# A four-layer kernel: maxima spread by load, first keys moved by other queues, five products a quarter slot later

## What is computed

```python
x = x + cross_attention(layernorm(x), ctx, tau, delta)   # 16 heads of 16, ctx has 1601 rows
x = x + top1_of_8_experts(layernorm(x))                   # router, all 8 experts, the best one kept
x = x + window_attention(ctx, layernorm(x))               # scores in a window, context, tanh(cat @ W_c.T)
x = x + slots(layernorm(x))                               # gelu, top 8 of 64 slots, slots updated once

# cross attention:
scores = einsum('blhe,bshe->bhls', qh, kh) * tau + delta
a = softmax(scores / sqrt(16)); out = einsum('bhls,bshd->blhd', a, vh) @ Wo.T + bo
```

## Time and profile before

| | us |
|---|---|
| three runs | 1069.53, 1071.1, 1069.47 |
| median | 1069.53 |
| the profiled execution | 1072.81 |
| its span, first to last instruction | 1070.8 |
| TensorE busy in it | 980.2 (92%) |
| VectorE busy | 742.4 (69%) |
| ScalarE busy | 572.9 (54%) |
| GpSimd busy | 64.5 (6%) |

### The profile page before, as it was taken

How to read it: one execution, slowest core, us unless ns; L and a number is a source line. 1 busy time by engine, 2 the same in 40 slices (tenths; PEclk the granted TensorE clock), 3 DMA queues, 4 the chain that set the end, 5 groups by cost and what they waited for, 6 DMA issues and landing times.

```text
span 1070.8 us, 13621 instructions
## 1 busy us (share of the span) xinstructions
PE 980.2 (92%) x4794; PEld 389.6 (36%) x4794; DVE 742.4 (69%) x1704; ACT 572.9 (54%) x1063; POOL 64.5 (6%) x91
## 2 busy tenths in 40 slices
PE   7699999999899999889899989889899989889886
PEld 3353322233333334323333334323333334234643
DVE  5589888887777777767677687777677774126633
ACT  3366666666455456656455456656455466740330
POOL 3351000000000000000000000000000000100000
PEclk9899999999999999989899999999899899899899
DMA  7946500001000000001000000001000000040032
GB/s 190 190 88 112 123 1 16 16 2 35 1 16 1 15 1 11 6 1 55 1 16 1 16 1 13 4 1 55 1 16 1 1 1 21 21 127 1 1 98 79
DMA packets 34411, 36.19 MB, mean 34 GB/s; under 512 B 6766, under 2 KB 31387, under 8 KB 34083
## 3 DMA queue, kind: packets, MB, share of 16 engines
q1 hardware_dynamic: 33102, 34.43, 13.1%
q10 hardware_dynamic: 1162, 0.64, 0.4%
q0 software_dynamic: 80, 0.26, 0.1%
HBM read 21.55 MB, written 7.35 MB: 27 GB/s over the span
## 4 chain that ended last, share of the span: by engine, by line
issue 48%; PE 31%; DVE 8%; DMA 4%; SPq 3%; ACT 2%; POOL 2%; DVEq 1%; POOLq 0%; ACTq 0%
PE ps_o L1168 8%; PE ps_m L1084 8%; PE ps_e L1370 5%; DVE mx L1671 4%; DMA xres<-in_x 1%; PE ps_e L1041 1%; PE ps_m L1370 1%; SPq L558 1%; DMA q_stack<-probs 1%; PE ps_m L1188 1%; DMA d_parts<-delta_parts 1%; PE ps_m L1318 1%; POOL rstd L701 1%; POOL xres L753 1%; ACT probs L867 1%
## 5 line engine op out<-in xcount | busy, mean ns | idle before, releaser
L1671 DVE TENSOR_REDUCE mx<-ps_m 128x1 f32<-128x401 f32 x1024 | 536.1, 568 | 186.0 <-PE ps_m L1084 177.4
L867 ACT ACTIVATE probs<-ps_e 128x512 f32<-128x512 f32 (+1 forms) x763 | 438.3, 598 | 325.1 <-PE ps_e L1370 323.2
L1084 PE MATMUL ps_m<-k_stack,q_stack 99*128 99x401 bf16 x1024 | 318.6, 343 | 36.5 <-DVE mx L1671 27.0
L1370 PE MATMUL ps_e<-q_stack,k_stack 101*128 101x512 bf16 (+1 forms) x763 | 298.6, 393 | 11.2 <-ACT probs L867 9.4
L1168 PE MATMUL ps_o<-probs,v_heads 128*32 128x512 f32 (+1 forms) x1664 | 232.2, 632 | 0.0
L1370 PEld LDWEIGHTS ps_e<-q_stack,k_stack 101*128 101x128 bf16 (+1 forms) x763 | 75.5, 100 | 264.6 <-ACT probs L867 172.4
L1084 PEld LDWEIGHTS ps_m<-k_stack,q_stack 99*128 99x128 bf16 x1024 | 101.6, 99 | 183.0 <-DVE mx L1671 123.5
L1272 PE MATMUL ps_m<-expert_w,xnT 128*128 128x512 f32 x192 | 98.4, 593 | 0.7 <-DVE xb L1809 0.7
L1168 PEld LDWEIGHTS ps_o<-probs,v_heads 128*32 128x32 f32 (+1 forms) x1664 | 33.4, 109 | 62.7 <-issue 49.8
L867 ACT ACTIVATE probs<-ps_m 128x512 f32<-128x512 f32 (+1 forms) x69 | 41.5, 601 | 15.6 <-PE ps_m L1370 15.6
L1809 DVE SCALAR_TENSOR_TENSOR xb<-ps_m,hot,xb 128x256 f32<-128x256 f32 x84 | 40.6, 483 | 7.8
(11 more groups left out here) (333 smaller groups left out, 730.7 us busy)
## 6 DMA issues: line engine op xcount, KB each, us to landing
q_stack<-q_parts SPq DMA_DIRECT2D x78, 64.0 KB, 2.6
expert_w<-in_expert_wT SPq DMA_DIRECT2D x2, 1024.0 KB, 12.9
xres<-in_x SPq DMA_DIRECT2D x4, 512.0 KB, 3.8
x<-xres SPq DMA_DIRECT2D x4, 512.0 KB, 3.0
probs<-x SPq DMA_DIRECT2D x1, 2048.0 KB, 8.7
...
```

Of the source, the lines that this page charges most:

```text
L867: act.activation(probs[0:n, k % 2, h, :], score_bank(c, k, h)[0:n, :], ACT.Exp).then_inc(s["exp_done"], 1)
L1084: pe.matmul(ring_bank((n1, u))[:, 0:SPLIT], qst[0:MAX_ROW, g, h, P * t:P * t + P], kst[0:MAX_ROW, HG * g + h, QUARTER_START[q]:QUARTER_STA ...
L1370: pe.matmul(score_bank(c, k, h)[0:n, :], kst[0:ROWS, HG * g + h, P * st:P * st + n], qst[0:ROWS, g, h, :], start=True, stop=True).then_inc ...
L1671: dve.tensor_reduce(mx[:, q, col:col + 1], ring_bank((n1, u))[:, 0:SPLIT], AX.X, ALU.max)\
```

## The change

It has three parts.

1. **Maxima by load.** `units_of` gets the chunk. Chunk 0 keeps the even spread; chunks 1 to 3 take the table `BY_LOAD`, 2 to 7 units a slot, still 256 in all, and `BY_QUARTER` splits them over the quarters. `max_end`, `units_at` and `M_AT` follow. In chunks 1 to 3 the groups' turned maxima come in quarters 45, 89, 145 and 193 (before: 45, 97, 149 and 201).
2. **Five products later.** The lags of `y0`, `router`, `score0`, `z0` and `h` go from 3 to 4, and all that follows a job moves with it: `e0` from quarter 38 to 40, `t2a` from 117 to 119, `aTa` from 137 to 140, `t3a` from 170 to 174, `logits` from 181 to 186, `alphaT` from 199 to 204.
3. **The first keys' moves.** SyncE loses the ones, the delta's store and the delta's load; ScalarE issues the store behind step `D`; GpSimd issues the ones of the queries, the delta's load, and two of the six row moves of the first and the second key piece; ScalarE keeps none of these two. The ones of the maximum rows go on GpSimd inside the loop, behind step `L` 2. The masks go from the end of `START` to unit 8 of the loop.

```diff
-GATHER_SP = ((0, 4, 2, 1, 5, 3), (0, 4, 2, 1), (0, 4, 2))
-GATHER_ACT = ((), (5, 3), (1, 5, 3))
+GATHER_SP = ((0, 4, 2, 1), (0, 4, 2, 1), (0, 4, 2))
+GATHER_POOL = ((5, 3), (5, 3))
+GATHER_ACT = (1, 5, 3)
...
-         ("K", 3, 0), ("V", 0), ("V", 1), ("G", 2)]
-START += [("V", i) for i in range(2, V_EARLY)] + [("L", 1), ("U",)]
-BESIDE = []
+         ("K", 3, 0), ("V", 0), ("V", 1), ("G",)]
+START += [("V", i) for i in range(2, V_EARLY)] + [("L", 1)]
+BESIDE = [(8, ("U",))]
...
+BY_LOAD = [4, 5, 3, 5, 7, 2, 2, 7, 7, 2, 7, 4, 7,
+           7, 5, 4, 6, 6, 6, 6, 6, 6, 6, 6, 4, 6,
...
+BY_QUARTER = {2: (1, 0, 1, 0), 3: (1, 0, 1, 1), 4: (1, 1, 1, 1), 5: (1, 2, 1, 1), 6: (1, 2, 1, 2), 7: (2, 2, 1, 2)}
...
-JOBS = [("ota", None, 10, 3), ("otb", "ota", 2, 3), ("y0", "otb", 3, 3), ("y1", "y0", 2, 3), ("t1a", "y1", 11, 3),
-        ("t1b", "t1a", 2, 3), ("router", "t1b", 3, 2), ("e0", "router", 5, 6)]
+JOBS = [("ota", None, 10, 3), ("otb", "ota", 2, 3), ("y0", "otb", 4, 3), ("y1", "y0", 2, 3), ("t1a", "y1", 11, 3),
+        ("t1b", "t1a", 2, 3), ("router", "t1b", 4, 2), ("e0", "router", 5, 6)]
...
-            sp.wait_ge(s["delta_parts"], 1)
-            sp.dma_start(d_parts.rearrange("a (p s) -> p a s", s=P), delta3[:]).then_inc(s["delta_stored"], 16)
-            sp.wait_ge(s["delta_stored"], 16)
...
+            pool.wait_ge(s["delta_stored"], 16)
+            pool.dma_start(kst[DELTA_ROW:DELTA_ROW + 3, 0:3 * HG, :], d_parts[:, 0:S].unsqueeze(1).broadcast_to((3, 3 * HG, S)))\
+                .then_inc(s["ld_delta_k"], 16)
+            for i, rows in enumerate(GATHER_POOL):
+                first_col, end_col, last_block = KEY_PIECES[i]
+                pool.wait_ge(s["blk_parts"], BLOCK[last_block] + 1)
+                for j, row in enumerate(rows):
+                    move_k(pool, 0, (row,), k_soft[len(rows) * i + j], first_col, end_col)
```

More of the change, by code:

```diff
@@ L182, in ring_numbers @@
             k, h = divmod(q, HG)
-            order += [(NG * c + j, u) for j, u in units_at(k, h) if wanted(NG * c + j)]
-            if q in M_AT and wanted(NG * c + 1 + M_AT.index(q)):
-                order.append(("m", NG * c + 1 + M_AT.index(q)))
+            order += [(NG * c + j, u) for j, u in units_at(c, k, h) if wanted(NG * c + j)]
+            if q in M_AT[c] and wanted(NG * c + 1 + M_AT[c].index(q)):
+                order.append(("m", NG * c + 1 + M_AT[c].index(q)))
             if q in O_AT and (c or q > O_AT[0]):
@@ L401, in build @@
         k_half = [sem(f"k_half{i}") for i in range(2)]
+        k_soft = [sem(f"k_soft{i}") for i in range(4)]
         q_loaded = [sem(f"q_loaded{g}") for g in range(NG)]
@@ L528, in block_cols, with wait_first_keys @@
             return k_cols[BLOCKS[b][1]][1] if BLOCKS[b][0] == "K" else CT
+        def wait_first_keys(eng, half):
+            if half == 0:
+                eng.wait_ge(k_half[0], 16 * sum(len(rows) for rows in GATHER_SP[:2]))
+                for moved in k_soft:
+                    eng.wait_ge(moved, 16)
+            else:
+                eng.wait_ge(k_half[1], 16 * K_PARTS)
         def k_loads(g):
@@ L628, in _ @@
                 sp.wait_ge(q_stored[m], 16 * NC)
-            for i, half in enumerate(k_half):
-                sp.wait_ge(half, 16 * K_PARTS * HALF_OF_PIECE.count(i))
+            for i in range(2):
+                wait_first_keys(sp, i)
             sp.wait_ge(k_loaded[1], 16 * K_PARTS)
@@ L1894, in chunk @@
                     for h in range(HG):
-                        for j, u in units_at(k, h):
+                        for j, u in units_at(c, k, h):
                             if wanted(NG * c + j):
```

62 lines of the change are left out of this document (33 added, 29 removed), and 2 rows, old and new, of the table BY_LOAD.

## The result

| | before | after |
|---|---|---|
| median of 20 runs, us | 1070.22 | 1064.60 |
| ratio of the runs, 95% interval | 1 | 0.9933 [0.9913, 0.9953] |
| the profiled execution, us | 1072.81 | 1067.79 |
| before chunk 0, us | 89.6 | 94.3 |
| chunks 0, 1, 2, 3, us | 160.2, 237.8, 238.0, 224.8 | 161.0, 231.9, 231.9, 225.2 |

The change made the kernel 0.67% faster. The forecast was 1040 us in a range from 1028 to 1058: wrong by 25 us, and outside the range. The sign was right, the sum was not. The 20 runs of after lie between 1056.3 us (granted clock 0.976) and 1071.2 us (0.958), and their times mostly follow that clock; those of before lie between 1068.0 and 1075.7.

What follows compares the result with a forecast made beforehand. In a chunk VectorE or TensorE, whichever needs more, sets the pace; the start waits on SyncE's issue order. Load 13, later products 8 and first keys' moves 8.6 sum to 29.6 us off 1069.5: 1040 us, range 1028 to 1058.

Steps and rivals of the forecast that it cites:

- third rival: At the start: transfers bind, first maximum product at 32.1 us, the start pays 2.3; 1046 us, chance 0.11.
- the larger of the two is the least that the stretch can take: In a stretch of slots: counts times prices per engine, VectorE or TensorE; the larger is its least time; net 18.3 us.
- The first rival: Chunks 1 to 3: short slots bare the chains, full ones jam; load pays 2, later products 5; 1054 us, chance 0.20.
- The fourth rival: Slots of seven maxima, chunks 1 to 3: VectorE and TensorE take turns, 1.0 us lost each, 1078 us; chance 0.05.
- the slower one: The fourth rival: VectorE and TensorE take turns in slots of seven maxima, 1078 us; chance 0.05.

Runs made afterwards that it cites:

- the mends: Changed kernel with queries' ones behind the first root and masks back in START: 1052.9 us; with the maximum rows' ones on SyncE too: 1049.6 us.
- the mended start: Changed kernel with masks back in START, queries' ones behind the first root, maximum rows' ones on SyncE: 1049.6 us; with even maxima 1058.5 us.
- best_h: Changed kernel with masks back in START, queries' ones behind the first root, and h at its old lag of 3: 1053.3 us, ratio 0.9830 to before.
- h_three: Changed kernel with the start of before and h at its old lag of 3: 1058.8 us, ratio 0.9869 to before.

## Why the prediction was wrong

**The first keys' moves: forecast -8.6 us, measured +4.8.** The part on SyncE's queue was right: the queries' moves go when their parts are ready (26.34 us in the kernel after, issued at 26.37), and the first maximum product no longer waits for a move. Two steps failed. First, the ones on GpSimd were priced as issue time only ("about 1 us ahead of memsets that nothing waits for so early"). Behind the memsets stands the drain that opens the first root, and the root began only when the transfer had landed, at 11.9 us. The earlier trace rows could not show it: there GpSimd's first transfer comes behind the root. The step should have asked for each queue what waits behind the moved transfer, the landing included; as it was, the query chain, which sets the first maximum, came 3.8 us late (16.33 to 20.09). The third stop is the same mistake on a line that the prediction did not price at all: the maximum rows' ones on GpSimd inside the loop. Second, the masks were priced at 3.0 us from their rows at the end of START, of which 2 would be paid. Beside GpSimd's work in the loop they took 5.4, the stop was 4.56 us with three banks as the only cover, and half clock followed it. With the three causes removed chunk 0 begins at 79.6 to 80.6 us, against 87.2 to 89.6 with the start of before: 7 to 10 us, around the forecast of 8.6 and inside its ends of 2 to 10.6. The size of the gain was read rightly, and what stands in its way was not; but it is another start than the one priced, with the masks in `START` and one more transfer on SyncE's queue, so that the close agreement is partly luck.

**Transfers bind the start (third rival).** Refuted. Moves spaced by the transfers would have put the first maximum at 32.1 us; with the mends it starts at 28.83 to 28.87 us, without a wait for a move. The rule of the Trainium skill beside which the rival stood ("DMA: Bandwidth & Descriptors", section "Issuing engines are not separate DMA queues") is not refuted by that: that the engines share 16 DMA engines no run here contradicts, and the issue order was what held the queries.

**Five products a quarter later: forecast -8 us, measured -6.0 (2.4 more or less).** Right in mechanism, and in size within the interval. In the trace of after the product follows the work ahead of it at once.

**Maxima by load: forecast -13 us, measured -2.2 alone (2.7 more or less), -4.8 (3.6) beside the lags, and -9 (3.5) beside the lags on the mended start.** The step that failed is "the larger of the two is the least that the stretch can take", used as if differences of that least were differences of the time. It holds where the stretch ran near its sum before: slots 5 and 6, 9.27 us against 9.53. Slots 30 to 34 ran 21.57 us against a sum of 18.8, with VectorE busy for 16.8, as this window of the kernel before shows:

```profile
389.20:410.77 21.57, 19.67 (x114) 8.58 (x110) 16.78 (x36) 14.22 (x31) 0.00 (x0) 1.00 0.00 1
```

There something else set the pace, and the 2.2 us were not VectorE's to give. (The sum itself has a slip: the stretches that take maxima, -0.4 + 1.9 + 0 + 0.3 + 1.7 + 0.5, add up to 4.0 us more and not 3.8, which changes nothing.) The full slots cost more than their sum: 2.82 for 1.7 in slots 35 to 39, 0.84 for nothing in 14 to 21. The first rival, balance on paper only, had put this term at 2 and the later products at 5; the load and lags alone were 2.2 and 6.0. Its time of 1054 us missed mainly since it took the start at full gain. The fourth rival, engines that take turns, did not come: the slots 35 to 39, five of seven maxima, cost 1.1 us more than forecast, 0.2 a slot; its point was 0.8.

**Chunk 3: forecast -4.3 on paper by the load and a third of the later products' 8, measured +0.4.** Windows of slots 47 to 51 of chunk 3, of the kernel before and of the kernel after:

```profile
934.36:950.37 16.01, 13.95 (x70) 3.42 (x70) 1.86 (x5) 11.42 (x24) 0.00 (x0) 0.95 0.00 0
```

```profile
924.55:944.16 19.61, 18.25 (x70) 3.63 (x70) 2.11 (x6) 11.37 (x23) 0.00 (x0) 0.66 0.00 0
```

3.6 us of the gain were given back there, with the same 70 products at a clock of 0.66 and of 0.95. The prediction priced what the later lags do at the end of a chunk at nothing (0.5 us without cover). By the pattern above, ten kernels of ten with `h` at 4, this loss goes with the change; that it is the lag's is not shown, as best_h took 2.7 us more than h_three there without it.

**The chances** put 0.92 on faster, and faster it was. The fault of the range was that every case, the slower one too, kept a gain at the start: none had a cost in a queue to which work was moved.
